# One-hots of the slot list: one fused VectorE operation per token tile and choice, and no scaling on ScalarE

## The chip, the cores and the metric

The kernel runs on one core of a Trainium2 chip. The metric is the device time of one execution in microseconds (us); before the change the median of three runs is 830.17 us (828.87 to 830.80).

## What is computed

The input `x` is 64 samples of 64 rows by 512 (4096 tokens of 512 values). Each sample is first multiplied by a 64x64 matrix that an index per sample selects, plus a bias. The result goes through a mixture-of-experts layer with 16 routed experts, four of them per token, and one shared expert, and is added to `x`:

```python
h = einsum('bct,bcd->bdt', x, w[subjects]) + b[subjects][:, :, None]      # 4096 tokens x 512
scores = sigmoid(h @ gate_weight.T)                                      # 16 experts
# two of four groups by their top two biased scores, then the top four experts in them
w = 2.5 * scores[sel] / (scores[sel].sum(-1) + 1e-20)
out = sum_e w_e * (silu(h @ gate_e.T) * (h @ up_e.T)) @ down_e.T
shared = (silu(h @ shared_gate.T) * (h @ shared_up.T)) @ shared_down.T
return x + out + shared
```

## The kernel before

Everything is laid out in tiles of 128 tokens (`NT` = 32 tiles). The five engine programs are written out by hand, each in its own order, and meet by semaphores. There are three stages.

1. **Subjects and logits** (to about 50 us). TensorE multiplies each sample's rows by its matrix, turns the results and computes the gate's logits.
2. **Shared expert and routing** (about 50 to 192 us). All 32 tiles go through the shared expert in eight groups of four tiles. The loop over n = 0 to 31 (`shared_step` of each engine) has four parts per group: two products of 12 matmuls each and the down product of the previous group's first tile in parts 0 and 1, its other three down products in part 2, two more products in part 3. Beside it VectorE works through the routing, part by part (`ROUTE_STEPS`, line 63): who goes to which expert, the sizes, the slots, and the instruction words for the third stage.
3. **Routed experts** (192 us to the end). The tokens are gathered by expert into 143 tiles (`NR`), each goes through its expert, and the results are added to the output. The gathers are GpSimd's indirect DMAs, and need the index of every slot, `idx_all`.

**The slot list.** The change touches how `idx_all` comes about. Each token has four slots (one for each chosen expert); a slot number is a tile and a lane (0 to 127). `slot_places` (line 1557) cuts the slot numbers into `slot_tile` (number of a pair of tiles, 0 to 71, `NRD` = 72), `slot_lane` and `slot_scale` (1 or 6144, for the even and the odd tile of the pair). The inverse list (which token sits in which slot) is made by TensorE: for each of 32 token tiles and 4 choices one matmul of a one-hot matrix of lanes (128 tokens x 128 lanes, times the token's number) with a one-hot matrix of pairs (128 tokens x 72, times `slot_scale`), all summed in `psM`.

The one-hots are made in 16 groups (`N_GROUPS`) of 2 token tiles (`ENTRIES`), which is 8 matmuls (`PAIRS`) each. They lie in rings of four groups: `entry` for the pairs, and `lane1h` for the lanes, a view into `x_ring`, under whose name it appears in the trace. Three engines take part, and three tables by n (lines 67 to 72) say in which step of the shared expert:

- VectorE, `make_entries(g)` (line 1572): three operations on the whole group, with both operands full tensors (one of them broadcast): the comparison of pairs (576 elements per partition, line 1590), that of lanes (1024, line 1591), and the factor on the pairs (576, line 1594). `ENTRY_STEPS` has group 0 to 3 in steps 12 to 15 and two groups in each of steps 16 to 21. From group 4 on it waits for `table_done` of the group that had the ring's place.
- ScalarE, `scale_lanes(g)` (line 910): two activations of 512 elements (line 917) that multiply the lane one-hots by the token's number, in place. `SCALE_STEPS` has them in steps 13 to 21, behind the other work of the step.
- TensorE, `fill_slots(g)` (line 1118): the 8 matmuls (line 1126). `FILL_STEPS` has them in steps 14 to 22, behind the step's other matmuls; it waits for `entry_ready`.

In step 23 `fill_idx` (line 1597) waits for all 16 fills and makes `idx_all`, for which GpSimd's first gather waits.

What else VectorE does in a group of four steps: the low part of each activation tile (`split_shared_x`, line 1628, four times), the product of gate and up (`shared_mix`, line 1636, twice), the low part of the hidden tile (`split_shared_hid`, line 1642, twice), and now and then the low part of a piece of weights (`split_low`, line 1293). TensorE waits for each of these within the group or one step later. ScalarE copies the high parts (lines 759 and 843), does the silu (line 838) and copies results out of PSUM (`copy_y`, line 826); `psY` has two banks, so TensorE's down product (line 1156) waits for the copy of the one before the last.

## Time and profile before

| | |
|---|---|
| median of 3 runs | 830.17 us |
| profiled execution | 830.59 us |
| its span in the trace | 828.8 us |
| TensorE busy (matmul) | 813.5 us, 98% of the span |
| VectorE, ScalarE, GpSimd busy | 483.4, 408.3, 437.0 us |
| mean granted clock of TensorE | 0.998 of 2.4 GHz |

The span is the time from the first to the last instruction of the trace; the execution's own time is 1.8 us longer. A matmul's duration runs from its start to its modelled end, and matmuls overlap, so 98% busy does not mean that none starts late: what a late start costs is read from the starts of neighbouring matmuls. In the same way two VectorE operations in a row overlap: a start may lie some 0.08 us before the end of the one in front, and what an operation costs in a row of many is the distance between starts.

### The profile page before, as it was taken

Reading aid. Unit: us, or ns where it says so; the run is one execution under the profiler, and the core shown is the slowest. Engines: PE = TensorE matmul, PEld = TensorE weight load, DVE = VectorE, ACT = ScalarE, POOL = GpSimd, SP = SyncE. Lnnn points to the kernel's source line nnn. Section 1 sums busy time; section 2 is a strip of 40 time slices with the busy share of each in tenths; the row PEclk is TensorE's granted clock in tenths of the full one; section 3 lists DMA queues with packets and bytes.
Section 4 is the critical chain, followed back from the end, with each engine's and each line's share of the span. In section 5 each row is a group of like instructions: output and inputs, shape, how many; then the busy total and the mean of one; then the engine's idle time right before and its main releaser. Section 6 shows DMA issues by size and latency. Waiting matters only on the chain.

```text
span 828.8 us, 19394 instructions
## 1 busy us (share of the span) xinstructions
PE 813.5 (98%) x4136; PEld 651.2 (79%) x4137; DVE 483.4 (58%) x1007; ACT 408.3 (49%) x815; POOL 437.0 (53%) x400
## 2 busy tenths in 40 slices
PE   9999999999999999999999999999999999999996
PEld 5578877788888888888888888888888888878784
DVE  5788887736544445744457446747567466464541
ACT  4864467635444335543356335546455355354431
POOL 5503111527367666566655666565664675756433
PEclk9999999999999999999999999999999999999999
DMA  8985967799999999899998999899998998999845
GB/s 292 390 327 174 248 146 211 163 251 242 214 262 236 212 191 205 184 271 250 183 202 184 268 220 213 202 280 199 244 270 202 261 239 212 248 194 179 155 63 73
DMA packets 145304, 181.50 MB, mean 219 GB/s; under 512 B 30571, under 2 KB 103923, under 8 KB 142835
## 3 DMA queue, kind: packets, MB, share of 16 engines
q0 software_dynamic: 37776, 89.08, 52.3%
q1 hardware_dynamic: 106528, 80.45, 37.9%
q10 hardware_dynamic: 834, 10.49, 3.3%
q14 instruction: 149, 1.21, 0.5%
q8 instruction: 17, 0.28, 0.2%
HBM read 82.52 MB, written 67.17 MB: 181 GB/s over the span
## 4 chain that ended last, share of the span: by engine, by line
PE 90%; issue 3%; ACT 2%; DVE 2%; DVEq 1%; POOLq 0%; POOL 0%; ACTq 0%; SPq 0%
PE psGU L1098 45%; PE psY L1098 23%; PE psY L1156 4%; PE psH L975 4%; PE psGU L1139 3%; PE psGU L1141 3%; PE psGU L1140 3%; PE psT L975 2%; PE psY L1024 1%; PE psH L1001 1%; ACT x_ring L917 1%; PE psGU L1024 1%; PE psM L961 0%; PE psM L1126 0%; ACT xT_pair L759 0%
## 5 line engine op out<-in xcount | busy, mean ns | idle before, releaser
L1098 PE MATMUL psGU<-split_w,xT_pair 128*128 x1716 | 414.1, 390 | 0.0
L1098 PEld LDWEIGHTS psGU<-split_w,xT_pair 128*128 128x128 f32 x1716 | 321.9, 188 | 69.1 <-issue 0.7
L682 POOL DMA_INDIRECT out<-y_ring,idx_all x143 | 230.5, 1612 | 200.0 <-SPq L569 177.8
L1697 DVE SCALAR_TENSOR_TENSOR aT<-aT,w_ring,psGU 128x256 f32<-128x256 f32 x143 | 68.5, 479 | 241.5 <-ACT aT L930 143.0
L1098 PE MATMUL psY<-split_w,hidT_hi 128*128 x572 | 190.1, 413 | 0.2 <-issue 0.2
L677 POOL DMA_INDIRECT tok_ring<-h_rows,idx_all x143 | 150.9, 1055 | 74.5 <-issue 42.3
L930 ACT ACTIVATE aT<-psGU 128x256 f32<-128x256 f32 x143 | 55.0, 385 | 251.6 <-PE psGU L1098 187.0
L826 ACT ACTIVATE y_ring<-psY 128x512 f32<-128x512 f32 x173 | 103.3, 599 | 91.1 <-PE psY L1098 43.8
L1098 PE MATMUL psY<-split_w,hidT_lo 128*128 x286 | 112.6, 394 | 0.0
L1098 PEld LDWEIGHTS psY<-split_w,hidT_hi 128*128 128x128 f32 x572 | 96.9, 189 | 13.2 <-issue 0.5
L1682 DVE STREAM_TRANSPOSE psT<-x_ring 128x512 f32<-128x512 f32 x143 | 102.4, 716 | 1.0 <-DMA w_ring<-tok_ring 1.0
L1616 DVE TENSOR_TENSOR xT_pair<-psT,xT_pair 128x512 fp32r<-128x512 f32 x143 | 97.3, 680 | 2.6 <-issue 2.2
L743 ACT ACTIVATE xT_pair<-psT 128x512 fp32r<-128x512 f32 x143 | 86.5, 605 | 1.0 <-DVE psT L1682 1.0
L690 POOL DMA_DIRECT2D out<-y_ring x32 | 29.7, 1191 | 94.8 <-ACT y_ring L826 93.1
L1710 DVE TENSOR_TENSOR split_w<-raw_w,split_w x42 | 51.4, 1223 | 32.7 <-ACT split_w L894 23.8
L1098 PEld LDWEIGHTS psY<-split_w,hidT_lo 128*128 128x128 f32 x286 | 53.7, 188 | 12.2
L1688 DVE TENSOR_TENSOR hidT_lo<-psH,hidT_hi 128x256 fp32r<-128x256 f32 x143 | 59.6, 417 | 1.4 <-issue 1.0
L817 ACT ACTIVATE hidT_hi<-psH 128x256 fp32r<-128x256 f32 x143 | 54.3, 380 | 4.2 <-PE psH L975 2.5
L975 PEld LDWEIGHTS psH<-ident,aT 128*128 128x128 f32 x286 | 39.8, 140 | 20.6 <-DVE aT L1697 1.2
L975 PE MATMUL psH<-ident,aT 128*128 128x128 f32 x286 | 54.6, 272 | 0.8 <-DVE hidT_lo L1688 0.8
L894 ACT ACTIVATE split_w<-raw_w x42 | 44.6, 1062 | 6.6 <-issue 2.0
L1140 PE MATMUL psGU<-split_w 128*128 128x512 f32 x96 | 37.5, 391 | 0.0
(241 smaller groups left out, 667.5 us busy)
## 6 DMA issues: line engine op xcount, KB each, us to landing
x_ring<-tok_ring SPq DMA_DIRECT2D x284, 128.0 KB
raw_w<-ffn_w SPq DMA_DIRECT2D x17, 1536.0 KB, 9.7
out<-y_ring POOLq DMA_DIRECT2D x32, 256.0 KB
x_ring<-x_pairs SPq DMA_DIRECT2D x12, 512.0 KB, 8.3
h_rows<-tok_ring SPq DMA_DIRECT2D x16, 256.0 KB, 9.1
h_rows<-y_ring SPq DMA_DIRECT2D x16, 256.0 KB, 9.2
tok_ring<-h_rows,idx_all POOLq DMA_INDIRECT x143
out<-y_ring,idx_all POOLq DMA_INDIRECT x143
```

The source lines that it names most:

```text
L677: pool.indirect_dma_start(tok_ring[:, r % RING, :], None, h_rows[:, :], bass.IndirectOffsetOnAxis(idx_all[:, r:r + 1], 0)).then_inc(gather ...
L682: pool.indirect_dma_start(out[:, :], bass.IndirectOffsetOnAxis(idx_all[:, r:r + 1], 0), y_ring[:, r % YRING, :], None, compute_op=ALU.add) ...
L743: act.activation(xT_hi[:, t.slot % 2, :], psT[t.slot % 2][:], ACT.Copy).then_inc(xhi_ready, 1)
L826: act.activation(y_ring[:, s, :], psY[t.slot % 2][:], ACT.Copy).then_inc(y_ready, 1)
L930: act.activation(silu[:, t.slot % 2, :], psGU[t.slot % 2][:, 0:I], ACT.Silu).then_inc(silu_ready, 1)
L975: mm = pe.transpose(dst[:, k * P:(k + 1) * P], src[:, k * P:(k + 1) * P], ident[:])
L1098: mm = pe.matmul(dst, a[:, slot, c], w(at + col + k * H), start=(k == 0 and a is high and at == 0), stop=(k == parts - 1 and a is low))
L1140: pe.matmul(as_low, split_w[:, w:w + P], low, start=False, stop=False)
L1616: v.tensor_tensor(xT_lo[:, t.slot % 2, :], psT[t.slot % 2][:], xT_hi[:, t.slot % 2, :].bitcast(F32), ALU.subtract).then_inc(xT_ready, 1)
L1682: v.transpose(psT[t.slot % 2][:].rearrange("p (k b j) -> p k j b", k=HK, j=QUADS), x_duo[:, t.slot // DUO_TILES, :, t.slot % DUO_TILES, :] ...
L1688: v.tensor_tensor(hidT_lo[:, t.slot % 2, :], psH[:, 0:I], hidT_hi[:, t.slot % 2, :].bitcast(F32), ALU.subtract).then_inc(hidT_ready, 1)
L1697: v.scalar_tensor_tensor(out=hid[:, half, :], in0=gate, scalar=w_ring[:, w_slot, bass.ds(expert, 1)], in1=up, op0=ALU.mult, op1=ALU.mult). ...
```

## The change

- `make_entries(g)` now issues 16 tensor-scalar operations for a group, two for each of its 8 pairs of token tile and choice: `lane_no` (0 to 127) compared with the token's lane and multiplied by the token's number (128 elements), and `pair_no` (0 to 71) compared with the token's pair and multiplied by its `slot_scale` (72 elements). The two values per partition of each operation are `[P, 1]` columns of tables in SBUF. There is no wait between them; the last one of a group raises `entry_ready`.
- ScalarE's `scale_lanes` and the semaphore `places_ready` are gone; `entry_ready` counts groups.
- The tables `slot_pair`, `slot_lane`, `slot_scale` are now float32, the one-hots are still float16. In both rings the one-hot of a pair is now contiguous (before, two were interleaved element by element).
- `lane_no` and `pair_no` hold half as much as `lane_q` and `tile_q`.

```diff
--- before.py
+++ after.py
@@ -52,7 +52,6 @@
 LAST_PIECE = (2 * SPLITS - 1) * PIECES - 1
 ENTRIES = 2
 PAIRS = ENTRIES * TOPK
-DUO = 2
 ENTRY_RING = 4
 X_CHUNK = 4
 BIG = 3.0e38
@@ -66,8 +65,6 @@
                16: ("read_words",), 23: ("fill_idx",), 24: ("read_sp_words",)}
 ENTRY_STEPS = {12: (0,), 13: (1,), 14: (2,), 15: (3,), 16: (4, 5), 17: (6, 7), 18: (8, 9), 19: (10, 11),
                20: (12, 13), 21: (14, 15)}
-SCALE_STEPS = {13: (0,), 14: (1,), 15: (2, 3), 16: (4, 5), 17: (6, 7), 18: (8, 9), 19: (10, 11), 20: (12, 13),
-               21: (14, 15)}
 FILL_STEPS = {14: (0,), 15: (1,), 16: (2, 3), 17: (4, 5), 18: (6, 7), 19: (8, 9), 20: (10, 11), 21: (12, 13),
               22: (14, 15)}
 N_GROUPS = NT // ENTRIES
@@ -160,8 +157,8 @@
         key16 = sb("key16", [P, E])
         group_c = sb("group_c", [P, BC, NG])
         iota_tile = sb("iota_tile", [P, NRP])
-        lane_q = sb("lane_q", [P, P, DUO], F16)
-        tile_q = sb("tile_q", [P, NRD, DUO], F16)
+        lane_no = sb("lane_no", [P, P], F16)
+        pair_no = sb("pair_no", [P, NRD], F16)
         token_no = sb("token_no", [P, NT])
         warm = sb("warm", [P, 1])
         pad_rows = sb("pad_rows", [P, NRP])
@@ -230,7 +227,7 @@
         in_cw = home(cw_ring[:].rearrange("p s c -> p (s c)"), RING * P)
         in_x = home(x_ring[:].rearrange("p s h -> p (s h)"), RING * H)
         lane1h = in_x([P, ENTRY_RING * PAIRS * P // 2]).bitcast(F16).rearrange(
-            "p (s d l q) -> p s d l q", s=ENTRY_RING, l=P, q=DUO)
+            "p (s q l) -> p s q l", s=ENTRY_RING, l=P)
 
         mask = in_raw([P, NB, LEAD + BC, E])
         masked = sb("masked", [P, BE])
@@ -293,14 +290,13 @@
         slot_e = cond_sb
         slot_i = sb("slot_i", [P, NT, TOPK], I32)
         part_i = sb("part_i", [P, 3, NT * TOPK], I32)
-        slot_tile = sb("slot_tile", [P, NT * TOPK], F16)
-        slot_lane = sb("slot_lane", [P, NT * TOPK], F16)
-        slot_scale = sb("slot_scale", [P, NT * TOPK], F16)
+        slot_pair = sb("slot_pair", [P, NT * TOPK])
+        slot_lane = sb("slot_lane", [P, NT * TOPK])
+        slot_scale = sb("slot_scale", [P, NT * TOPK])
         with nc.sbuf_tensor("entry_high", [P, ENTRY_RING * PAIRS * NRP // 2], F32R) as entry_high:
             pass
         entry_flat = sb("entry", [P, ENTRY_RING * PAIRS * NRP], F16)
-        entry = entry_flat[:, 0:ENTRY_RING * PAIRS * NRD].rearrange("p (s d n q) -> p s d n q", s=ENTRY_RING,
-                                                                    d=PAIRS // DUO, q=DUO)
+        entry = entry_flat[:, 0:ENTRY_RING * PAIRS * NRD].rearrange("p (s q n) -> p s q n", s=ENTRY_RING, n=NRD)
         in_cw_late = home(cw_ring[:].rearrange("p s c -> p (s c)"), RING * P)
         table_both = in_cw_late([P, NRD, 2])
         table = table_both.rearrange("p n q -> p (n q)")[:, 0:NR]
@@ -358,7 +354,6 @@
         words_ready = sem("words_ready")
         sp_words_summed = sem("sp_words_summed")
         sp_words_ready = sem("sp_words_ready")
-        places_ready = sem("places_ready")
         entry_ready = sem("entry_ready")
         table_done = sem("table_done")
         slots_ready = sem("slots_ready")
@@ -633,8 +628,8 @@
 
             def entry_consts():
 
-                iota(lane_q[:], [[1, P], [0, DUO]], 0, 0)
-                iota(tile_q[:], [[1, NRD], [0, DUO]], 0, 0)
+                iota(lane_no[:], [[1, P]], 0, 0)
+                iota(pair_no[:], [[1, NRD]], 0, 0)
                 pool.sem_inc(consts, 1)
 
             def clear_pads():
@@ -876,8 +871,6 @@
                     shared_hid_highs(g, 0)
                 else:
                     shared_silu(g, 1)
-                for e in SCALE_STEPS.get(n, ()):
-                    scale_lanes(e)
                 if n in HIGHS:
                     split_ahead(n)
                 if n in X_COPIES:
@@ -906,16 +899,6 @@
                             act.sem_inc(act_clear, 1)
                         act.sem_inc(act_clear, 1)
                     act.sem_inc(act_clear, 1)
-
-            def scale_lanes(g):
-
-                act.wait_ge(places_ready, 2 * (g + 1))
-                s = g % ENTRY_RING
-                half = PAIRS // DUO // ENTRIES
-                for k in range(ENTRIES):
-                    lanes = lane1h[:, s, k * half:(k + 1) * half, :, :].rearrange("p d l q -> p (d l q)")
-                    act.activation(lanes, lanes, ACT.Copy, scale=token_no[:, g * ENTRIES + k:g * ENTRIES + k + 1]
-                                   ).then_inc(entry_ready, 1)
 
             def step(t, n, j):
                 if n == NT:
@@ -1117,13 +1100,12 @@
 
             def fill_slots(g):
 
-                pe.wait_ge(entry_ready, ENTRIES * (g + 1))
+                pe.wait_ge(entry_ready, g + 1)
                 if g == 0:
                     pe.wait_ge(pos_read, NB)
                 s = g % ENTRY_RING
                 for q in range(PAIRS):
-                    d, half = q // DUO, q % DUO
-                    mm = pe.matmul(psM[:, 0:NRD], lane1h[:, s, d, :, half], entry[:, s, d, :, half],
+                    mm = pe.matmul(psM[:, 0:NRD], lane1h[:, s, q, :], entry[:, s, q, :],
                                    start=(g == 0 and q == 0), stop=(g == N_GROUPS - 1 and q == PAIRS - 1),
                                    skip_group_check=True)
                 mm.then_inc(table_done, 1)
@@ -1562,7 +1544,7 @@
                 ts(part_i[:, 1, :], flat, P - 1, None, ALU.bitwise_and)
                 ts(part_i[:, 2, :], flat, P, None, ALU.bitwise_and)
                 settle()
-                put(v.tensor_copy(slot_tile[:], part_i[:, 0, :]))
+                put(v.tensor_copy(slot_pair[:], part_i[:, 0, :]))
                 put(v.tensor_copy(slot_lane[:], part_i[:, 1, :]))
                 put(v.tensor_copy(slot_scale[:], part_i[:, 2, :]))
                 settle()
@@ -1578,21 +1560,13 @@
                 if g >= ENTRY_RING:
                     v.wait_ge(table_done, g - ENTRY_RING + 1)
                 s = g % ENTRY_RING
-                pairs = slice(g * PAIRS, (g + 1) * PAIRS)
-
-                def duos(ap, n):
-                    return ap.rearrange("p (d q) -> p d q", q=DUO).unsqueeze(2).to_broadcast(
-                        [P, PAIRS // DUO, n, DUO])
-
-                def every(ap):
-                    return ap.unsqueeze(1).to_broadcast([P, PAIRS // DUO, ap.shape[1], DUO])
-
-                put(v.tensor_tensor(entry[:, s], every(tile_q[:]), duos(slot_tile[:, pairs], NRD), ALU.is_equal))
-                v.tensor_tensor(lane1h[:, s], every(lane_q[:]), duos(slot_lane[:, pairs], P), ALU.is_equal
-                                ).then_inc(places_ready, 1)
-                settle()
-                v.tensor_tensor(entry[:, s], entry[:, s], duos(slot_scale[:, pairs], NRD), ALU.mult
-                                ).then_inc(places_ready, 1)
+                for q in range(PAIRS):
+                    n, at = g * ENTRIES + q // TOPK, slice(g * PAIRS + q, g * PAIRS + q + 1)
+                    v.tensor_scalar(lane1h[:, s, q, :], lane_no[:], slot_lane[:, at], token_no[:, n:n + 1],
+                                    ALU.is_equal, ALU.mult)
+                    made = v.tensor_scalar(entry[:, s, q, :], pair_no[:], slot_pair[:, at], slot_scale[:, at],
+                                           ALU.is_equal, ALU.mult)
+                made.then_inc(entry_ready, 1)
 
             def fill_idx():
```

**VectorE, step 13** (group 1; `ties`, `cw_ring`, `e_cols`, `raw_col` belong to the shared expert and the routing; `x_ring` is the lane one-hots). Before:

```order
L1628 TENSOR_TENSOR split_w<-kept_w,xT_pair 128x512
L1636 TENSOR_TENSOR ties<-ties,psGU 128x512
L1238 TENSOR_TENSOR cw_ring<-e_rows,ident 16x192
L1238 TENSOR_TENSOR raw_prod<-sp_raw,ident 16x16
L1500 TENSOR_REDUCE e_cols<-cw_ring 16x12
L1501 TENSOR_REDUCE raw_col<-raw_prod 16x1
L1590 TENSOR_TENSOR entry<-tile_q,slot_tile 128x576
L1591 TENSOR_TENSOR x_ring<-lane_q,slot_lane 128x1024
L1594 TENSOR_TENSOR entry<-entry,slot_scale 128x576
```

and now (line numbers of the changed kernel; the last two rows come eight times in a row):

```order
L1602 TENSOR_TENSOR split_w<-kept_w,xT_pair 128x512
L1610 TENSOR_TENSOR ties<-ties,psGU 128x512
L1220 TENSOR_TENSOR cw_ring<-e_rows,ident 16x192
L1220 TENSOR_TENSOR raw_prod<-sp_raw,ident 16x16
L1482 TENSOR_REDUCE e_cols<-cw_ring 16x12
L1483 TENSOR_REDUCE raw_col<-raw_prod 16x1
L1565 TENSOR_SCALAR x_ring<-lane_no,slot_lane,token_no 128x128
L1567 TENSOR_SCALAR entry<-pair_no,slot_pair,slot_scale 128x72
```

The group stands at the same place; three operations have become sixteen, each with two operands of one value per partition. Steps 16 to 21 have two groups each, and so 32 in a row.

**ScalarE, steps 17 and 18** (`aT` to `hidT_hi` are the shared expert's, `out<-x` is a DMA that ScalarE issues). Before:

```order
L759 ACTIVATE tok_high<-kept_w 128x512 x2
L826 ACTIVATE y_ring<-psY 128x512
L917 ACTIVATE x_ring<-x_ring,token_no 128x512 x4
L732 DMA out<-x 16x16384
L826 ACTIVATE y_ring<-psY 128x512 x3
L843 ACTIVATE hidT_hi<-aT 128x512
L917 ACTIVATE x_ring<-x_ring,token_no 128x512 x4
```

and now:

```order
L754 ACTIVATE tok_high<-kept_w 128x512 x2
L821 ACTIVATE y_ring<-psY 128x512
L727 DMA out<-x 16x16384
L821 ACTIVATE y_ring<-psY 128x512 x3
L838 ACTIVATE hidT_hi<-aT 128x512
```

The scaling that stood between the copies of `psY` is gone, and nothing took its place on this engine.

## Rows read from the trace of the kernel before

**Rows 1.** The page: busy time by engine, and granted TensorE clock in 40 slices

```profile
PE 813.5 (98%) x4136; PEld 651.2 (79%) x4137; DVE 483.4 (58%) x1007; ACT 408.3 (49%) x815; POOL 437.0 (53%) x400
...
PEclk9999999999999999999999999999999999999999
```

**Rows 2.** Waits of TensorE over the span: us in total, times, longest us

```profile
PE psY L1156 <- ACT y_ring L826: 2.6, 3, 1.2
...
PE psM L1126 <- ACT x_ring L917: 0.9, 1, 0.9
```

**Rows 3.** Table of stretches: length, then busy time (instructions) of each engine

```profile
104.00:125.00 21.00, 20.15 (x123) 15.08 (x123) 17.98 (x44) 14.11 (x24) 3.47 (x4) 1.00 0.63 159
125.00:153.50 28.50, 25.85 (x190) 19.96 (x189) 20.87 (x42) 22.90 (x40) 6.08 (x7) 1.00 0.67 188
153.50:192.00 38.50, 38.50 (x168) 31.39 (x168) 16.78 (x29) 15.85 (x27) 17.95 (x16) 1.00 1.00 211
```

**Rows 4.** Timeline of TensorE at its largest waits and at the last fill

```profile
106.09 0.39 PE L1156 MATMUL psY<-split_w,aT_low 128*128 128x512 f32 x1
107.33 0.50 PE L1156 MATMUL psY<-split_w,hidT_hi 128*128 128x512 f32 x1 [0.85 <-ACT y_ring L826]
...
149.70 0.39 PE L1156 MATMUL psY<-split_w,aT_low 128*128 128x512 f32 x1
151.25 0.73 PE L1156 MATMUL psY<-split_w,hidT_hi 128*128 128x512 f32 x2 [1.17 <-ACT y_ring L826]
...
152.75 0.72 PE L1126 MATMUL psM<-entry,x_ring 128*128 128x72 f16 x16
```

**Rows 5.** Groups of instructions, 100 to 160 us: busy us, mean ns, idle before

```profile
L917 ACT ACTIVATE x_ring<-x_ring,token_no 128x512 f16<-128x512 f16 x32 | 21.0, 714 | 4.9 <-DVE entry L1594 4.9
...
L690 POOL DMA_DIRECT2D out<-y_ring x12 | 10.6, 939 | 50.6 <-ACT y_ring L826 50.6
```

**Rows 6.** Timeline of VectorE: group 0 of the one-hots

```profile
104.00 0.46 DVE L1590 TENSOR_TENSOR entry<-tile_q,slot_tile 128x576 f16<-128x576 f16 x1
...
104.98 0.45 DVE L1594 TENSOR_TENSOR entry<-entry,slot_scale 128x576 f16<-128x576 f16 x1
105.35 0.68 DVE L1628 TENSOR_TENSOR split_w<-kept_w,xT_pair 128x512 fp32r<-128x512 f32 x1
```

**Rows 7.** Timeline of VectorE: its waits, and the end of the last group

```profile
117.48 0.69 DVE L1628 TENSOR_TENSOR split_w<-kept_w,tok_high 128x512 fp32r<-128x512 f32 x1 [1.73 <-ACT tok_high L759]
...
124.37 0.69 DVE L1636 TENSOR_TENSOR aT<-aT,psGU 128x512 f32<-128x512 f32 x1 [1.12 <-PE psGU L1141]
...
137.53 0.69 DVE L1636 TENSOR_TENSOR aT<-aT,psGU 128x512 f32<-128x512 f32 x1 [3.13 <-PE psGU L1141]
140.81 0.69 DVE L1628 TENSOR_TENSOR split_w<-kept_w,xT_pair 128x512 fp32r<-128x512 f32 x1 [2.59 <-ACT xT_pair L759]
...
149.18 1.22 DVE L1293 TENSOR_TENSOR split_w<-raw_w,split_w 128x1024 fp32r<-128x1024 f32 x1
```

**Rows 8.** Timeline of VectorE: tensor-scalar operations with one, no and two [P,1] operands

```profile
84.82 0.51 DVE L1244 TENSOR_SCALAR cw_ring<-cw_ring,n 128x16 f32<-128x16 f32 x3
...
102.05 0.17 DVE L1247 SCALAR_TENSOR_TENSOR e_rows<-e_rows,cw_ring 128x16 f32<-128x16 f32 x1
102.13 0.17 DVE L1244 TENSOR_SCALAR cw_ring<-e_rows 128x16 f32<-128x16 f32 x1
...
110.01 0.60 DVE L1244 TENSOR_SCALAR x_ring<-iota_tile,e_cols 16x143 f32<-16x143 f32 x2
110.54 0.69 DVE L1242 TENSOR_SCALAR x_ring<-iota_tile,e_cols 16x144 f32<-16x144 f32 x3
```

**Rows 9.** Instructions of line 1244: duration ns min/median/max, first and last start

```profile
L1244 DVE TENSOR_SCALAR cw_ring<-e_rows x2: 164/166/168, 102.0 to 102.1; 128x16 f32<-128x16 f32 x2
...
L1244 DVE TENSOR_SCALAR slot_scale<-slot_scale x1: 195/195/195, 97.6 to 97.6; 128x128 f16<-128x128 f16 x1
...
L1244 DVE TENSOR_SCALAR cw_ring<-cw_ring x1: 234/234/234, 154.8 to 154.8; 128x143 f32<-128x143 f32 x1
```

## The prediction

> **What bounds the kernel now.** I read the page first: TensorE is busy for 98% of the span, at full clock in every slice, and VectorE and ScalarE for 58% and 49% [rows 1]. The few waits that TensorE has come next: almost all of them are for two lines of ScalarE, 2.6 us for the copy of `psY` and 0.9 us for the scaling of lanes [rows 2]. They lie between 104 and 153.5 us, where the one-hots are made; from 153.5 us to the start of the routed experts TensorE has no gap (38.50 of 38.50 us) [rows 3]. So what the change is worth is decided in this stretch. A delay of the last fill delays everything behind it, since nothing later has slack on TensorE.
>
> The timeline shows the waits. At 107.33 us a down product starts 1.24 us after the matmul in front of it, at 151.25 us one starts 1.55 us after it [rows 4]; the usual step is 0.23 us (168 matmuls in 38.5 us) [rows 3], so these two cost 1.0 and 1.3 us. The profile's idle times are 0.16 us too short per wait, because a matmul's modelled end (0.39 us) outlasts its step. All four together are 2.6 + 0.9 + 4 x 0.16 = 4.1 us. That is what the ScalarE half of the change can give back, and no more. Why ScalarE is late: its 32 scalings take 21.0 us [rows 5] in these 50 us, and in the second part it is busy for 22.90 of 28.50 us [rows 3].
>
> **The two sides of the change.**
>
> ScalarE loses 21.0 us of work [rows 5]. It was the late engine at all four waits, so 4.1 us go if nothing else becomes late.
>
> TensorE's 128 small matmuls read contiguous one-hots now, before strided ones. Sixteen of them took 0.56 us (they start at 152.75 and the profile gives the last one's end at 0.72 us [rows 4]; less 0.16 us for the end). At most I allow 0.5 us over all groups, either way, and take 0, because TensorE is going to wait here (below).
>
> GpSimd makes two smaller constants before 50 us, where nothing waits for them: 0.
>
> VectorE is the question. A group of one-hots cost it 105.35 - 104.00 = 1.35 us [rows 6]. Now a group is 16 operations on 128 or 72 elements, each with two `[P, 1]` operands. The trace has no such float16 operation, but all its parts:
> - No such operand, 16 elements: 102.13 - 102.05 = 0.08 us from start to start [rows 8].
> - One such operand, 16 elements: three in a row take 0.51 us and one of them 0.23, so the distance is (0.51 - 0.23) / 2 = 0.14 us [rows 8].
> - Two, 143 elements: two operations start at 110.01 and the next line at 110.54, so 0.265 us each [rows 8]. Of this the length is (143 - 16) elements; without such operands these cost 234 - 166 = 68 ns in float32 [rows 9]. That leaves 0.20 us for 16 elements.
>
> So each `[P, 1]` operand adds 0.06 us to the distance, and it is not hidden behind the operation in front. In float16 the length costs less: 128 elements take 195 ns against 166 ns for 16 float32 ones [rows 9], so 29 ns. The lane operation is then 0.20 + 0.03 = 0.23 us and the pair operation 0.20 + 0.01 = 0.21 us. A group takes 8 x (0.23 + 0.21) = 3.5 us against 1.35. The bounds: if the `[P, 1]` operands were wholly hidden, 8 x (0.11 + 0.09) = 1.6 us. If float16 gave no gain over one element per cycle (twice the float32 slope of 68 ns for 127, some 1.07 ns per element), 8 x (0.32 + 0.26) = 4.6 us. I take 3.5, as its nearest rows are those with two such operands, and they were read three operations in a row.
>
> The Trainium skill speaks against this price: its page "VectorE: DVE Perf Modes", section on the TRN2 errata, has 58 cycles plus a quarter of the elements for such an operation from SBUF to SBUF. That would be 0.094 and 0.079 us, and 1.4 us for a group. The row with two operands (0.265 us) is over twice what that formula gives for it, with half of its 143 elements (0.135 us), so I go by the row.
>
> **The sum.** VectorE makes the first group from 104.00 us on and is done with the last one at 149.18 us, when its next operation starts [rows 6, 7]. These 45.2 us hold 16 x 1.35 = 21.6 us of one-hots and four waits of 1.73 + 1.12 + 3.13 + 2.59 = 8.6 us [rows 7]; the other 15.0 us are shared expert and routing. With 3.5 us a group, one-hots take 56 us. The waits for TensorE (1.12 and 3.13) go, since TensorE is ahead then. The two for ScalarE's copy shrink but stay, at about 1.3 us each: VectorE writes a product, ScalarE copies twice (0.6 us each), and only then can VectorE go on. The last group is done at 104.0 + 15.0 + 2.6 + 56 = 177.6 us; TensorE's last fill started at 153.03 us before (sixteen matmuls from 152.75 on [rows 4], the second eight 0.28 us later), and now the last one at 177.6. That is **24.6 us later**.
>
> Does TensorE get there earlier, or later by itself? Its own work in steps 13 to 22 ended at 153 us with 4.1 us of waits, so it needs some 45 us for what takes VectorE 73. It can be ahead of VectorE by one step only, because each step's fills need the one-hots of the step before. The ring of four groups does not hold VectorE up: it asks for fills of the step before, which are done by then. GpSimd's first gather waits for the slot list; that list comes one step after the last fill as before, and from there the 38.5 us without a gap [rows 3] move as a whole. I take nothing back later.
>
> 830.59 + 24.6 = 855.2 us for the profiled execution. Its own time lies 0.4 us over the median of the three runs (830.17), so the forecast is **854.8 us**. Each 0.1 us more or less on a group is 1.6 us.
>
> **The rivals.**
>
> *The operands are hidden and it gets faster.* This is the one on the other side. Its place is the distance between two of the new operations. If the read of the next operation's `[P, 1]` values runs beside the operation in front, a group costs 1.6 us. The skill's formula above would come out here too. VectorE is done with the last group by 104.0 + 15.0 + 2.6 + 16 x 1.6 = 147.2 us, before TensorE, free of ScalarE's delays, wants it (153.0 - 4.1 = 148.9 us). TensorE gains the whole 4.1 us: 826.1 us. It decides up to (148.9 - 121.6) / 16 = 1.7 us a group. For it: VectorE has 8.6 us of waits to fill. Against it: the rows with one operand (0.14 against 0.08 us) and with two. Chance 9%.
>
> *A price between.* At 2 to 2.8 us a group the loss is -0.1 to +13 us: 830 to 843 us. It needs half of the read hidden, for which no row speaks. Chance 4%, a good part of it within 0.2%.
>
> *More than the price.* At 3.9 us a group (half the gain of float16), it is +31 us; at 4.6 us, +42: 861 to 873 us. Two mechanisms would add to 3.5 as well. TensorE waits up to 3 us at a time, over twice as long as now; its clock is full through waits of 1.3 us [rows 1, 2], and longer ones are not in this trace. At half clock (0.46 us a matmul as an estimate from the 0.23) the 72 matmuls of four steps take 33 us, about what VectorE needs for the same steps (8 groups of 3.5 and 5 of its own), so it would cost a few us only. The other is GpSimd. Its 12 accumulating DMAs of this stretch take 0.94 us each to issue [rows 5]; if VectorE's new operations could not run beside them, that is up to 11 us, for 866 us. The Trainium skill has that rule (page "SBUF — State Buffer", section "SBUF: two separate sides", the box on "DVE blocks DMA"): a VectorE operation in a two-port mode and GpSimd's writing of descriptors lock each other out. No row of this trace shows VectorE held up by one. Chance of more than 4 us a group in effect, 17%.
>
> **The numbers.** The forecast (3.0 to 4.0 us a group, 847 to 863 us) has 70%, more than that 17%, a price between 4%, the faster case 9%. A range of 845 to 868 us holds the first and most of the second, about 80%. A measurement of this kernel can tell a difference of 0.2%, or 1.7 us, from none: faster 0.09, same 0.02, slower 0.89.
>
> **What would show it.** In the changed kernel's profile: the lane and pair operations at 0.23 and 0.21 us from start to start, some 0.3 us each in duration; VectorE busy nearly without a gap from 104 to 178 us; ScalarE without line 917's work and idle for half of the stretch; TensorE waiting there for the one-hots (line `psM`), some 29 us in all, and no longer for ScalarE; the first gather near 181 us. It is wrong if the distance between the new operations is under 0.12 us, or if TensorE's waits are short and the last fill starts near 149 us. The sum is wrong if the last fill is late by some 25 us and the end is not.

## The result and the profile after

The changed kernel takes 853.55 us (median of 5 runs, 851.05 to 855.02) against 830.80 us for the kernel before (5 runs of the same chip, 828.87 to 831.96): 22.75 us more, a ratio of 1.027 with a 95% interval of 1.0249 to 1.0291. The forecast was 854.8 us in a range of 845 to 868. The profiled execution took 851.05 us, with a span of 849.3 us.

The page of the changed kernel, its busy times and the granted clock in 40 slices [rows 1 before]:

```profile
PE 820.4 (97%) x4136; PEld 658.4 (78%) x4137; DVE 516.5 (61%) x1215; ACT 388.9 (46%) x783; POOL 433.9 (51%) x400
...
PEclk9999989899999999999999999999999999999998
```

VectorE has 33 us more of busy time, ScalarE 19 us less, and TensorE's clock is down to eight tenths in slices 6 and 8 (106 to 127 us and 149 to 170 us) and in the last one. TensorE's waits over the whole span (total us, times, longest; [rows 2] before):

```profile
PE psM L1108 <- DVE entry L1567: 14.4, 8, 3.0
PE psT L1045 <- DVE x_ring L1503: 3.0, 1, 3.0
```

The two waits for ScalarE are gone, as the change meant. In their place TensorE waits for VectorE's one-hots (`psM` is the fill, `entry` the pair one-hot), eight times and up to 3.0 us, and once for the tables of the instruction words (`psT`), which stand behind two groups on VectorE. The stretches [rows 3], cut at the new end of the one-hots:

```profile
104.00:125.00 21.00, 18.04 (x87) 13.34 (x85) 19.95 (x82) 4.15 (x8) 3.44 (x4) 0.84 0.47 101
125.00:153.50 28.50, 21.24 (x136) 16.44 (x136) 28.14 (x118) 7.78 (x13) 3.56 (x4) 0.91 0.62 185
153.50:178.00 24.50, 17.21 (x95) 13.04 (x94) 23.22 (x93) 7.05 (x12) 2.70 (x3) 0.82 0.36 74
```

VectorE is busy for 19.95, 28.14 and 23.22 of 21.0, 28.5 and 24.5 us: it sets the pace from 104 to 177 us. Behind the five engines' busy times stand the granted clock, the DMA's share and its GB/s: the clock is 0.84, 0.91 and 0.82 of full, where it was 1.00.

VectorE's timeline at the first group [rows 6] and at the end of the last [rows 7]:

```profile
103.98 0.32 DVE L1565 TENSOR_SCALAR x_ring<-lane_no,slot_lane,token_no 128x128 f16<-128x128 f16 x1
104.21 0.29 DVE L1567 TENSOR_SCALAR entry<-pair_no,slot_pair,slot_scale 128x72 f16<-128x72 f16 x1
104.42 0.31 DVE L1565 TENSOR_SCALAR x_ring<-lane_no,slot_lane,token_no 128x128 f16<-128x128 f16 x1
...
107.44 0.68 DVE L1602 TENSOR_TENSOR split_w<-kept_w,xT_pair 128x512 fp32r<-128x512 f32 x1
...
176.42 0.31 DVE L1567 TENSOR_SCALAR entry<-pair_no,slot_pair,slot_scale 128x72 f16<-128x72 f16 x1
176.63 1.23 DVE L1275 TENSOR_TENSOR split_w<-raw_w,split_w 128x1024 fp32r<-128x1024 f32 x1
```

From the start of a lane operation to the next start it is 0.22 to 0.23 us, from that of a pair operation 0.21; the first group takes 107.44 - 103.98 = 3.46 us, where it was 1.35. The last one ends at 176.63 us, where it was 149.18.

TensorE's last fill [rows 4] and the first matmuls of the routed experts, in the changed kernel:

```profile
176.78 0.43 PE L1108 MATMUL psM<-entry,x_ring 128*128 128x72 f16 x8 [1.66 <-DVE entry L1567]
...
215.84 2.47 PE L1081 MATMUL psGU<-split_w,xT_pair 128*128 x10
```

and the same first routed matmuls in the kernel before:

```profile
192.09 1.78 PE L1098 MATMUL psGU<-split_w,xT_pair 128*128 x7
```

The last fill starts 0.15 us after the last group is done, at 176.78 us instead of 153.03; the routed experts start at 215.84 us instead of 192.09. Both are 23.75 us later (153.03 is 152.75 and half of the sixteen matmuls' 0.56 us): nothing between them gives any of it back.

### The profile page after: what moved, and what is told of

Same layout as the page of the kernel before. It is cut to its first block, busy times and chain, and to the rows that moved or that the text cites. A ratio compares the mean times of both kernels' runs of the same rounds, so it can differ in the third digit from the quotient of the medians.

```text
span 849.3 us, 19570 instructions
## 1 busy us (share of the span) xinstructions
PE 820.4 (97%) x4136; PEld 658.4 (78%) x4137; DVE 516.5 (61%) x1215; ACT 388.9 (46%) x783; POOL 433.9 (51%) x400
## 4 chain that ended last, share of the span: by engine, by line
PE 87%; DVE 8%; DMA 3%; ACT 1%; issue 0%; POOLq 0%; POOL 0%; SPq 0%; ACTq 0%; DVEq 0%
PE psGU L1081 46%; PE psY L1081 23%; PE psH L958 4%; PE psY L1138 3%; DVE x_ring L1565 3%; PE psGU L1121 3%; DVE entry L1567 3%; PE psGU L1123 3%; PE psGU L1122 3%; DMA h_rows<-tok_ring 1%; DMA h_rows<-y_ring 1%; PE psT L958 1%; DVE split_w L1602 1%; PE psGU L1007 0%; DMA x_ring<-x_pairs 0%
## 5 line engine op out<-in xcount | busy, mean ns | idle before, releaser
L677 POOL DMA_INDIRECT out<-y_ring,idx_all x143 | 228.0, 1594 | 198.2 <-SPq L564 176.5
L672 POOL DMA_INDIRECT tok_ring<-h_rows,idx_all x143 | 152.7, 1068 | 76.4 <-issue 42.3
L1122 PE MATMUL psGU<-split_w 128*128 128x512 f32 x96 | 39.6, 413 | 0.0
```

The source lines that it names most:

```text
L672: pool.indirect_dma_start(tok_ring[:, r % RING, :], None, h_rows[:, :], bass.IndirectOffsetOnAxis(idx_all[:, r:r + 1], 0)).then_inc(gather ...
L677: pool.indirect_dma_start(out[:, :], bass.IndirectOffsetOnAxis(idx_all[:, r:r + 1], 0), y_ring[:, r % YRING, :], None, compute_op=ALU.add) ...
L1122: pe.matmul(as_low, split_w[:, w:w + P], low, start=False, stop=False)
```

## The experiments

My theory was the prediction's: each operand of one value per partition adds 0.06 us to the distance between two VectorE operations, sixteen operations with two of them each make a group cost 3.5 us, and VectorE so becomes the engine that the fills wait for. The rivals: a cost per instruction whatever its operands; TensorE's lower clock; GpSimd in VectorE's way; and that ScalarE's relief was worth nothing in the first place. Each run shares its runs of the kernel before with the others of its set: 829.34 us for the first four, 828.98 us for the last four.

### The price of an operation by itself

```diff
             split_hid(tile_at(LAST))
...
+            def series(size, source, first, second):
+                for k in range(1024 // max(size, P)):
+                    at = k * max(size, P)
+                    put(v.tensor_scalar(out16[:, at:at + size], source[:, 0:size], first, second,
+                                        ALU.is_equal, ALU.mult))
+                settle()
+            series(128, from16, 1.0, 2.0)
+            series(128, from16, a, 2.0)
+            series(128, from16, a, b)
+            series(72, from16, a, b)
+            series(16, from16, a, b)
+            series(128, above, a, b)
+            series(512, from16, 1.0, 2.0)
+            series(512, from16, a, b)
```

> The kernel before, with rows of equal VectorE operations added behind its last one (nothing else computes on it there): comparison and factor as tensor-scalar, 8 in a row per form, 2 for the forms of 512 elements. The time of the whole is of no interest, only the distance from start to start in each row. Theory (each [P, 1] operand adds 0.06 us that nothing hides): float16, 128 elements: 0.11 us with immediates, 0.17 with one such operand, 0.23 with two; 72 elements with two 0.21, 16 elements with two 0.20; float32 input, 128 elements, two: 0.26; 512 elements: 0.20 with immediates, 0.32 with two. Rival (the cost is per instruction, whatever its operands): all forms of 128 elements and less at some 0.2 us, also those with immediates. Second rival (the operands are read beside a long operation in front): the two forms of 512 elements are equally far apart.

VectorE's timeline in this run, cut so that each row is a pair or a triple of one form (`w_num` holds the two `[P, 1]` operands; the first row has immediates, the second one operand, the third and fourth two):

```profile
818.47 0.30 DVE L1831 TENSOR_SCALAR cond_sb<-scores 128x128 f16<-128x128 f16 x2
...
819.42 0.42 DVE L1831 TENSOR_SCALAR cond_sb<-scores,w_num 128x128 f16<-128x128 f16 x2
...
821.01 0.54 DVE L1831 TENSOR_SCALAR cond_sb<-scores,w_num 128x128 f16<-128x128 f16 x2
...
824.18 0.51 DVE L1831 TENSOR_SCALAR cond_sb<-scores,w_num 128x72 f16<-128x72 f16 x2
```

With immediates a pair lasts 0.30 us and one operation 0.19, so the distance is 0.11. With one operand (one lasts 0.25 us, the minimum of its line) it is 0.17, with two (one lasts 0.31) 0.23, and on 72 elements (0.29) 0.22; on 16 elements it is 0.20. The whole row of float32 inputs and the rows of 512 elements:

```profile
826.40 2.14 DVE L1831 TENSOR_SCALAR cond_sb<-above,w_num 128x128 f16<-128x128 f32 x8
828.58 0.49 DVE L1831 TENSOR_SCALAR cond_sb<-scores 128x512 f16<-128x512 f16 x2
829.11 0.73 DVE L1831 TENSOR_SCALAR cond_sb<-scores,w_num 128x512 f16<-128x512 f16 x2
...
828.78 0.28 DVE L1831 TENSOR_SCALAR cond_sb<-scores 128x512 f16<-128x512 f16 x1
829.11 0.41 DVE L1831 TENSOR_SCALAR cond_sb<-scores,w_num 128x512 f16<-128x512 f16 x1
```

Eight float32 ones and the wait behind them take 828.58 - 826.40 = 2.18 us, at most 0.27 each. On 512 elements the distance is 0.49 - 0.29 = 0.20 us with immediates and 0.73 - 0.41 = 0.32 with two operands. These distances are within 0.01 us of what was expected (the trace has one execution of this kernel, and each row stands in it once). The cost is not one per instruction, since immediates make it half, and it is not hidden by a long operation in front: it is 0.12 us for two operands at 512 elements as at 128.

### One half of the fusion at a time

Lanes only, pairs wide as before, no scaling on ScalarE:

```diff
...
+                put(v.tensor_tensor(entry[:, s], every(pair_no[:]), duos(slot_pair[:, pairs], NRD), ALU.is_equal))
                 for q in range(PAIRS):
                     n, at = g * ENTRIES + q // TOPK, slice(g * PAIRS + q, g * PAIRS + q + 1)
                     v.tensor_scalar(lane1h[:, s, q, :], lane_no[:], slot_lane[:, at], token_no[:, n:n + 1],
                                     ALU.is_equal, ALU.mult)
-                    made = v.tensor_scalar(entry[:, s, q, :], pair_no[:], slot_pair[:, at], slot_scale[:, at],
-                                           ALU.is_equal, ALU.mult)
-                made.then_inc(entry_ready, 1)
+                settle()
+                v.tensor_tensor(entry[:, s], entry[:, s], duos(slot_scale[:, pairs], NRD), ALU.mult
+                                ).then_inc(entry_ready, 1)
```

> Only the lanes are made in the new way (8 operations with two [P, 1] operands), the pairs in two wide operations as before; no scaling on ScalarE. Theory (VectorE's price of a group sets the time): 8 x 0.225 + 2 x 0.37 = 2.55 us a group; last group done at 104.0 + 17.4 + 16 x 2.55 = 162.2 us, 9 us later than before's last fill: 840 us. Rival (what costs is TensorE's lower clock through its waits): waits are shorter than 2 us here, so the clock stays up and the time is within 2 us of the kernel before.

838.26 us, a ratio of 1.0101 (1.0079 to 1.0123), 8.9 us over the kernel before. VectorE's first group, its next operation after the last group, and TensorE's last fill:

```profile
103.87 0.46 DVE L1574 TENSOR_TENSOR entry<-pair_no,slot_pair 128x576 f16<-128x576 f16 x1
104.25 1.88 DVE L1577 TENSOR_SCALAR x_ring<-lane_no,slot_lane,token_no 128x128 f16<-128x128 f16 x8
...
106.40 0.69 DVE L1614 TENSOR_TENSOR split_w<-kept_w,xT_pair 128x512 fp32r<-128x512 f32 x1
...
161.52 1.23 DVE L1277 TENSOR_TENSOR split_w<-raw_w,split_w 128x1024 fp32r<-128x1024 f32 x1
...
161.67 0.43 PE L1110 MATMUL psM<-entry,x_ring 128*128 128x72 f16 x8 [1.33 <-DVE entry L1580]
```

A group takes 2.53 us, the last ends at 161.52 us and the last fill starts at 161.67, 8.6 us later than before. The time follows the price of a group. The rival's premise did not hold: TensorE waited 1.9 us at most, and its granted clock still was 0.92 from 104 to 125 us and 0.94 from 125 to 153.5 us. But the last fill follows VectorE by 0.15 us here too.

Pairs only, lanes in one wide comparison and scaled by ScalarE:

```diff
...
-                put(v.tensor_tensor(entry[:, s], every(tile_q[:]), duos(slot_tile[:, pairs], NRD), ALU.is_equal))
                 v.tensor_tensor(lane1h[:, s], every(lane_q[:]), duos(slot_lane[:, pairs], P), ALU.is_equal
                                 ).then_inc(places_ready, 1)
-                settle()
-                v.tensor_tensor(entry[:, s], entry[:, s], duos(slot_scale[:, pairs], NRD), ALU.mult
-                                ).then_inc(places_ready, 1)
+                for q in range(PAIRS):
+                    at = slice(g * PAIRS + q, g * PAIRS + q + 1)
+                    made = v.tensor_scalar(entry[:, s, q, :], tile_q[:], slot_tile[:, at], slot_scale[:, at],
+                                           ALU.is_equal, ALU.mult)
+                made.then_inc(places_ready, 1)
```

> Only the pairs are made in the new way (8 operations with two [P, 1] operands); the lanes in one wide comparison, scaled by ScalarE as before. Theory: 0.60 + 8 x 0.21 = 2.28 us a group; VectorE alone is done at 104.0 + 17.4 + 16 x 2.28 = 157.9 us, 5 us late: 836 us, and up to 842 us as ScalarE's two scalings still stand behind each group and before ScalarE's next copies, for which VectorE waits. Rival (ScalarE's relief is what matters, VectorE has idle time to spend): within 2 us of the kernel before.

839.89 us, a ratio of 1.0130 (1.0108 to 1.0152), 10.6 us more. TensorE's waits, VectorE's first operation behind the last group, and TensorE's last fills:

```profile
PE psY L1155 <- ACT y_ring L825: 6.3, 3, 2.9
PE psM L1125 <- ACT x_ring L916: 5.9, 4, 1.8
...
159.41 1.23 DVE L1292 TENSOR_TENSOR split_w<-raw_w,split_w 128x1024 fp32r<-128x1024 f32 x1
...
162.92 0.69 PE L1125 MATMUL psM<-entry,x_ring 128*128 128x72 f16 x16
```

VectorE is done at 159.41 us, but the last fills start at 162.92 and some 163.2 us: here both lines of ScalarE stand in TensorE's waits, 12.2 us together. Each scaling now waits for a later group (ScalarE waits 18.3 us for the pairs, before 4.9) and holds up ScalarE's copies behind it. So the half that is cheaper for VectorE (2.28 us a group against 2.53) saves the kernel nothing; whether it is the dearer one, the overlapping intervals leave open. In the full change ScalarE has no scaling to wait with.

### ScalarE's half alone

The scaling can be taken off ScalarE without a dear group on VectorE. First, VectorE scales itself, in two wide operations:

```diff
...
-                v.tensor_tensor(lane1h[:, s], every(lane_q[:]), duos(slot_lane[:, pairs], P), ALU.is_equal
-                                ).then_inc(places_ready, 1)
+                put(v.tensor_tensor(lane1h[:, s], every(lane_q[:]), duos(slot_lane[:, pairs], P), ALU.is_equal))
                 settle()
-                v.tensor_tensor(entry[:, s], entry[:, s], duos(slot_scale[:, pairs], NRD), ALU.mult
-                                ).then_inc(places_ready, 1)
+                v.tensor_tensor(entry[:, s], entry[:, s], duos(slot_scale[:, pairs], NRD), ALU.mult)
+                half = PAIRS // DUO // ENTRIES
+                for k in range(ENTRIES):
+                    lanes = lane1h[:, s, k * half:(k + 1) * half, :, :].rearrange("p d l q -> p (d l q)")
+                    made = v.tensor_scalar(lanes, lanes, token_no[:, g * ENTRIES + k:g * ENTRIES + k + 1], None,
+                                           ALU.mult)
+                made.then_inc(entry_ready, 1)
```

> The kernel before, but VectorE scales the lanes itself, in two wide operations (512 elements, one [P, 1] operand) per group; ScalarE's scaling is gone. Theory: 0.37 + 0.60 + 0.37 + 2 x 0.27 = 1.88 us a group, VectorE done with the last at 104.0 + 17.4 + 30.1 = 151.5 us; TensorE's last fill 1 to 2 us earlier than before: 829.5 us. Rival (VectorE has only its 8.6 us of waits to spend, 16 x 0.53 = 8.5 us, and hits TensorE as well): 831 to 835 us. If ScalarE's scaling was not what TensorE waited for, 831 us as before.

831.66 us, a ratio of 1.0026 (1.0012 to 1.0041), 2.3 us more. So it went the way of the rival and not of the gain I expected. TensorE's largest wait, VectorE's first group (from 104.86 us on) from its third operation, and the operation behind its last group:

```profile
PE psM L1124 <- DVE x_ring L1595: 2.2, 3, 1.5
...
105.96 0.46 DVE L1591 TENSOR_TENSOR entry<-entry,slot_scale 128x576 f16<-128x576 f16 x1
106.33 0.61 DVE L1595 TENSOR_SCALAR x_ring<-x_ring,token_no 128x512 f16<-128x512 f16 x2
106.86 0.69 DVE L1630 TENSOR_TENSOR split_w<-kept_w,xT_pair 128x512 fp32r<-128x512 f32 x1
...
154.07 1.21 DVE L1291 TENSOR_TENSOR split_w<-raw_w,split_w 128x1024 fp32r<-128x1024 f32 x1
```

A group takes 2.0 us, not 1.88: the wait that the factor on the pairs has now includes the lanes' comparison just in front, 0.12 us that I had left out. With 2.0 us my sum gives 104.0 + 17.4 + 32 = 153.4 us, 0.4 us late. This execution also began the stretch 0.86 us later than the other. The waits for ScalarE are gone, and TensorE waits 2.2 us for VectorE instead. One more part is the clock, below.

Second, GpSimd scales, between its DMAs (its program gets `scale_lanes` as ScalarE had it, with `pool.tensor_scalar`; ScalarE's is left out):

```diff
+POOL_SCALES = {7: (0,), 8: (1,), 11: (2, 3, 4, 5), 12: (6, 7), 15: (8, 9, 10, 11, 12, 13), 16: (14, 15)}
...
+                for e in POOL_SCALES.get(n, ()):
+                    scale_lanes(e)
```

> The kernel before, but GpSimd scales the lanes (two operations of 512 elements per group), between its accumulating DMAs; VectorE's three wide operations stay, ScalarE is relieved as in the changed kernel. Theory (the ScalarE half is worth TensorE's 4.1 us of waits if VectorE's price stays at 1.35 us a group): 4 us faster than the kernel before, if GpSimd needs less than 3 us a group. Rival (GpSimd and VectorE hold each other up at their operations on SBUF): VectorE's wide operations grow beyond 0.45 and 0.68 us, and the time is that of the kernel before or more.

852.37 us, a ratio of 1.0286 (1.0247 to 1.0324). The condition of my theory did not hold. Groups of instructions from 100 to 180 us (busy us, mean ns):

```profile
L694 POOL TENSOR_SCALAR x_ring<-x_ring,token_no 128x512 f16<-128x512 f16 x32 | 60.0, 2023 | 12.4 <-DVE entry L1605 12.4
...
L1605 DVE TENSOR_TENSOR entry<-entry,slot_scale 128x576 f16<-128x576 f16 x16 | 8.5, 532 | 0.0
```

The 32 scalings keep GpSimd busy for 60.0 us, so 3.8 us a group (one lasts 2.02 us in the mean): GpSimd is now what the fills wait for, 17.3 us in all. The rival is there too, but small. The factor takes 0.53 us in the mean instead of 0.45 because three of the sixteen took 0.85 to 0.94 us, and two of the lanes' comparisons took 1.09 us; the others took as long as before. TensorE did not wait for VectorE here.

### A version that beats both

TensorE's waits before were for ScalarE. Its scalings can stand elsewhere, with no operation changed:

```diff
-SCALE_STEPS = {13: (0,), 14: (1,), 15: (2, 3), 16: (4, 5), 17: (6, 7), 18: (8, 9), 19: (10, 11), 20: (12, 13),
-               21: (14, 15)}
+SCALE_STEPS = {14: (1,), 15: (2, 3), 16: (4, 5), 17: (6,), 18: (8, 9), 19: (10, 11), 20: (12, 13), 21: (14,)}
+SCALE_BETWEEN = {14: 0, 18: 7, 22: 15}
...
                         for j in range(1, GROUP):
                             shared_y(g - 1, j)
+                            if n in SCALE_BETWEEN and j <= ENTRIES:
+                                scale_half(SCALE_BETWEEN[n], j - 1)
```

> The kernel before with the same operations, but ScalarE's scalings of groups 0, 7 and 15 moved out of the steps in front of the down products and put between the copies of psY that TensorE waits for. Theory (TensorE's waits come from the place of the scalings in ScalarE's order): the waits for the copy (2.6 us) shrink to some 1 us, 2 to 3 us faster than the kernel before. Rival (ScalarE is simply too full in this stretch): the same waits at other places, same time.

825.58 us, a ratio of 0.9957 (0.9937 to 0.9978), 3.4 us less than the kernel before. TensorE's wait in the stretch that is left, and its last fills:

```profile
PE psM L1132 <- ACT x_ring L919: 0.9, 1, 0.9
...
149.61 0.71 PE L1132 MATMUL psM<-entry,x_ring 128*128 128x72 f16 x16
```

The 2.6 us of waits for the copy of `psY` are all gone, and the last fills start at 149.61 us instead of 152.75; VectorE's first group began at the same time in both. The other idea is to exchange the two factors:

```diff
...
-                act.wait_ge(places_ready, 2 * (g + 1))
...
+                    act.wait_ge(places_ready, 2 * g + 1)
...
-                v.tensor_tensor(entry[:, s], entry[:, s], duos(slot_scale[:, pairs], NRD), ALU.mult
+                v.tensor_tensor(lane1h[:, s], lane1h[:, s], duos(slot_scale[:, pairs], P), ALU.mult
                                 ).then_inc(places_ready, 1)
...
-                    act.activation(lanes, lanes, ACT.Copy, scale=token_no[:, g * ENTRIES + k:g * ENTRIES + k + 1]
+                    act.activation(pairs, pairs, ACT.Copy, scale=token_no[:, g * ENTRIES + k:g * ENTRIES + k + 1]
                                    ).then_inc(entry_ready, 1)
```

> The factors are exchanged: ScalarE multiplies the pairs by the token's number (two activations of 288 elements per group, before 512), VectorE the lanes by slot_scale (1024 elements, before 576). VectorE 1.57 us a group, ScalarE 0.9 instead of 1.27. Theory: VectorE is still below 1.7 us a group and hidden, ScalarE is relieved by 6 us: 1 us faster than the kernel before. Rival: VectorE's 3.5 us more push its low parts of the shared expert late: 1 to 3 us slower.

827.27 us, a ratio of 0.9968 (0.9952 to 0.9984), 1.7 us less by the medians. Groups of instructions from 100 to 160 us, and TensorE's wait for ScalarE:

```profile
L917 ACT ACTIVATE entry<-entry,token_no 128x288 f16<-128x288 f16 x32 | 15.1, 528 | 8.1 <-DVE entry L1596 8.1
...
L1595 DVE TENSOR_TENSOR x_ring<-lane_q,slot_lane 128x1024 f16<-128x1024 f16 x16 | 10.8, 678 | 0.1
L1599 DVE TENSOR_TENSOR x_ring<-x_ring,slot_scale 128x1024 f16<-128x1024 f16 x16 | 10.8, 676 | 0.0
...
PE psY L1161 <- ACT y_ring L826: 1.3, 2, 0.8
```

ScalarE's share falls from 21.0 to 15.1 us, and VectorE carries 3.6 us more without TensorE waiting for it. The edit changes a second thing: ScalarE waits for VectorE's two comparisons only and no longer for its factor, so it can begin earlier. How much of the 1.7 us comes of that, no run tells apart. Both together:

> Both of the two changes before together. Theory: TensorE's waits nearly gone, 3 to 4 us faster than the kernel before. Rival (VectorE at 1.57 us a group is now the late engine): no better than with the order alone.

824.84 us, a ratio of 0.9934 (0.9909 to 0.9959), 4.1 us less by the medians. The two stretches of [rows 3]:

```profile
104.00:125.00 21.00, 21.00 (x128) 16.09 (x127) 19.38 (x56) 10.89 (x22) 3.44 (x4) 1.00 0.49 103
125.00:153.50 28.50, 28.50 (x205) 22.89 (x204) 26.67 (x51) 23.48 (x46) 6.02 (x7) 1.00 0.75 222
```

TensorE has no wait left in them (21.00 of 21.00 and 28.50 of 28.50 us). The profiled execution is the slowest of the six (828.58 us); it came to its first group 3.2 us later, at 107.23 us. From there to the last fills it took 44.2 us (151.38 - 107.23), against 48.8 us (152.75 - 104.00) in the kernel before: 4.6 us less, near the 4.1 us that the prediction had put as the most that ScalarE's half can give. Whether the exchange adds anything to the order alone, the overlapping intervals leave open.

## Why the prediction was right

**What bounds it.** The stretch from 104 us on decides, and a delay of the last fill goes through to the routed experts undiminished: 23.75 us at the fill and 23.75 us at the first routed matmul. Of the profiled execution's shift only 20.5 us are left at the end, as its routed stage took 633.5 us (849.3 - 215.84) against 636.7 us (828.8 - 192.09). The medians differ by 22.75 us. The five executions of either kernel lie 3 to 4 us apart, so I do not take these last 1 to 3 us for an effect of the change. One reading was too wide: "almost all" of TensorE's waits before were for ScalarE only within this stretch; over the whole span it is 3.5 of 7.3 us, the rest lies before 104 us or in the third stage.

**The price.** 3.5 us a group were forecast from three rows, 3.46 us measured, and the series by itself shows the three terms: 0.11, 0.17 and 0.23 us for none, one and two operands.

**The sum.** 15.0 + 2.6 us of other work and waits were expected between the groups; it is 176.63 - 103.98 - 16 x 3.46 = 17.3 us. The last fill was forecast at 177.6 us and came at 176.78. Of the 0.8 us, 0.6 are the price (16 x 0.04). VectorE's two waits for ScalarE's copies were put at about 1.3 us each and are 1.3 us each. ScalarE is busy for 19 of the 74 us, so it idles for three quarters of the stretch and not for half; nothing in the sum hangs on it. For the rival "a price between", 2 us a group gives a loss of 0.6 us by the same sum (24.6 - 16 x 1.5), not of -0.1.

**The rule against it.** The forecast had weighed 1.4 us a group by the formula of the Trainium skill, page "VectorE: DVE Perf Modes", section on the TRN2 errata. The row set against it (0.265 us) is 1.96 times what the formula gives for it (0.135 us), not "over twice"; that changes nothing. The series shows what the formula lacks: with two operands the distance is 0.23 us, and the formula's 0.094 us for this length lie near the 0.11 us of immediates.

**TensorE's waits and clock.** Here the prediction was only half right. I expected some 29 us of waits. The profile has 14.4 + 3.0 us, with 0.16 us for each of the nine some 19 us. The rest is the lower clock that I had named as a possibility: the shares 0.84, 0.91 and 0.82 of 21, 28.5 and 24.5 us make 20.7 us at half clock ((1 - share) / 0.5 of each), and so 10 us of lost work. By the profile it cost nothing at the end, since TensorE would have waited otherwise (no run tried it): VectorE has no wait for TensorE from 104 to 178 us, and the last fill follows VectorE by 0.15 us.

**GpSimd.** The rival with up to 11 us more did not come. One of GpSimd's DMA issues in the timeline, and VectorE's new operations at that time:

```profile
139.09 0.93 POOL L685 DMA_DIRECT2D out<-y_ring  x1 [6.75 <-ACT y_ring L821]
```

```profile
138.90 0.30 DVE L1565 TENSOR_SCALAR x_ring<-lane_no,slot_lane,token_no 128x128 f16<-128x128 f16 x1
139.12 0.28 DVE L1567 TENSOR_SCALAR entry<-pair_no,slot_pair,slot_scale 128x72 f16<-128x72 f16 x1
139.33 0.34 DVE L1565 TENSOR_SCALAR x_ring<-lane_no,slot_lane,token_no 128x128 f16<-128x128 f16 x1
```

The distances of 0.21 to 0.23 us are those of the other groups, and GpSimd's issues in this stretch take 0.86 to 0.93 us each, where they took 0.94 us in the mean before: neither engine is held up. The Trainium skill's page "SBUF — State Buffer", section "SBUF: two separate sides", says that of a VectorE operation in a two-port mode and an operation of GpSimd, the one that starts first holds the shared ports for its whole instruction, and the other blocks wholly; its box on "DVE blocks DMA" has GpSimd kept from writing descriptors meanwhile. No such block shows for these short operations.

For an operation of GpSimd that reads SBUF the same section has this lock against VectorE operations with two SBUF inputs as well. The run with GpSimd's scaling agrees in part only. Two scalings in a row there, and VectorE's operations at that time, all with two inputs:

```profile
138.46 4.49 POOL L694 TENSOR_SCALAR x_ring<-x_ring,token_no 128x512 f16<-128x512 f16 x2
```

```profile
138.44 0.44 DVE L1601 TENSOR_TENSOR entry<-tile_q,slot_tile 128x576 f16<-128x576 f16 x1
138.81 0.68 DVE L1602 TENSOR_TENSOR x_ring<-lane_q,slot_lane 128x1024 f16<-128x1024 f16 x1
139.41 0.85 DVE L1605 TENSOR_TENSOR entry<-entry,slot_scale 128x576 f16<-128x576 f16 x1
140.19 0.45 DVE L1601 TENSOR_TENSOR entry<-tile_q,slot_tile 128x576 f16<-128x576 f16 x1
```

GpSimd is in one of its scalings through all of this. One of the four operations takes 0.4 us more than usual; none is held up for the 2 us of a scaling, which the rule would give.

## What to carry to other kernels

Before many small operations take the place of a few wide ones, read the distance from start to start of operations with the same kinds of operands, not their duration and not the length alone: here two `[P, 1]` operands cost 0.12 us each time, more than the whole operation of 128 elements without them (0.11 us), and the fused operations took 3.46 us a group where two passes and a factor had taken 1.35. Ask which engine has the slack and how much: VectorE had 8.6 us, the change asked for 34. And where an engine is late only at a few places, look at the order of its work first: moving six activations gave 3.4 us, of the 4.1 us that I estimate for taking all 32 away at no price.

## What the runs showed of the hardware

TensorE's clock fell to half in the kernel where VectorE scales, with hardly a wait in front. Two stretches of that run, with the columns of [rows 3] (TensorE's busy time is the second number, the clock the one behind GpSimd's):

```profile
104.00:114.00 10.00, 10.00 (x52) 8.05 (x51) 9.69 (x32) 3.52 (x6) 3.44 (x4) 1.00 0.83 187
114.00:125.00 11.00, 11.00 (x72) 7.82 (x71) 9.59 (x24) 3.31 (x6) 0.00 (x0) 0.84 0.16 30
```

TensorE is busy for the whole of both. Between 114.6 and 116.9 us it did eighteen matmuls with one column of weights and eight fills of 72 columns; from 117.9 to 121.1 us each 512-column matmul took 0.43 us from start to start instead of 0.23. The same small matmuls stand in the kernel before, whose clock stayed full there in the profiled execution. In all twelve executions of that version the mean clock was 0.995 to 0.997, in the seventeen of the kernel before mostly 0.997 or 0.998, in two 0.995 and 0.996. The 3.2 us at half clock are 1.6 us of lost work of TensorE, an estimate. What decides it between the two kernels stays open; no run here was made for it.

GpSimd's multiplication of 512 float16 values per partition by a `[P, 1]` operand lasted 2.02 us in the mean, against 0.71 us on ScalarE and 0.26 us from start to start on VectorE.
